# Cross attention 0 of a Perceiver block: key and value projections as three float16 matmuls, and one maximum operation over both row halves

## The chip, the cores and the metric

The kernel runs on one core of a Trainium2 chip. The metric is the device time of one execution in microseconds (us), the median of several runs. TensorE does the matmuls, VectorE (DVE), ScalarE (ACT) and GpSimd (POOL) work beside it, SyncE (SP) issues the DMAs. Each engine executes its own list of instructions in order; semaphores connect the lists.

## The reference: what is computed

The model has six parts one after the other (two cross attentions, a linear and a rotary attention, two mixtures of experts). The change is in the cross attention of the first part. The latents `x` are 32 batches of 64 rows of width 128, the context `ctx_1024` is 32 batches of 1601 rows of width 128, and there are 16 heads of width 8:

```python
def _mha_cross(x, mem, in_w, in_b, out_w, out_b):
    B, L, D = x.shape          # 32, 64, 128; mem: 32, 1601, 128
    H = NHEAD                  # 16
    hd = D // H                # 8
    ...
    q = _split_heads(x @ wq.T + bq, H)
    k = _split_heads(mem @ wk.T + bk, H)
    v = _split_heads(mem @ wv.T + bv, H)
    scores = jnp.einsum('bhqd,bhkd->bhqk', q, k) * (1.0 / math.sqrt(hd))
    attn = jax.nn.softmax(scores, axis=-1)
    out = _merge_heads(jnp.einsum('bhqk,bhkd->bhqd', attn, v))
    return out @ out_w.T + out_b
```

Everything is float32 in the reference, so the kernel either multiplies in float32 or splits a float32 number in a high and a low half of two bytes each.

## The kernel before

`cross_attention_0` goes through 16 pairs of batches. A pair `i` has four units `v` (batch `b = v // 2`, half of the heads `v % 2`), a unit has seven steps `st` of 256 context rows. In the loop of TensorE a step holds, in this order:

- `maxima`: two bf16 matmuls (line 988, contraction of 64 rows each, one into bank 0 and one into bank 1) that make scores for the row maximum of the next unit. In the loop they run two steps ahead. The seventh has 65 columns for each group of heads (line 992).
- one piece of other work, all of which shares bank 7: in units 0 and 2 a chunk of the value projection (`values`, line 948; such a unit is called a value unit below), in units 1 and 3 a chunk of the key projection (`keys`, line 942; a key unit). Chunks are 512, 512, 512 and 65 context rows and go to steps 0 to 3. Step 4 has `final`, step 6 of a key unit has `queries` (line 955). `take_bank7` makes each wait for the reader of the one before.
- `mix` (line 1029), probabilities times values, which waits for the exponentials of ACT (line 1200);
- `scores` of two steps on (line 1009); after step 5 `shifts` (lines 964 and 965), which bring the maximum into the queries.

DVE follows in the same order: two maximum reductions for each step (line 1103, one for each bank), the spreading of the maximum (lines 1108 to 1116) and the result of the unit before (lines 1136, 1138) at step 4, the shifted queries (line 1122) after step 5, the bias of the queries (line 1090) at step 6 of a key unit, and the masking of the mix (lines 1127, 1130) ahead of the first reduction of the next unit. TensorE may write bank 0 again when the reduction of bank 0 is through, and bank 1 when that of bank 1 is:

```python
for rt in range(2):
    wait_if(eng, a_max, n * 14 + 2 * a + rt - 1)
```

ACT copies key and value chunks from bank 7 (lines 1184, 1193) between the exponentials. POOL splits keys into bf16 halves (lines 897, 899) and queries (904 to 911). SP loads the context and spreads the split keys over partitions (24 DMAs for each batch). The context `ctxT` is float32 and goes straight from its DMA into the projections. Projections of pair `i + 1` are made within pair `i`. The functions as they stand before the change:

## Time and profile before

| | before |
|---|---|
| median of 3 runs | 3556.06 us (3551.76 to 3568.44) |
| the profiled execution: its own time | 3552.84 us |
| its span from first to last instruction | 3551.1 us |
| TensorE busy | 3326.5 us, 94% |
| VectorE busy | 2495.5 us, 70% |
| ScalarE busy | 1909.4 us, 54% |
| GpSimd busy | 1102.6 us, 31% |
| mean granted TensorE clock | 0.964 of 2.4 GHz |

The whole program is one chain of stages on one core. The stage of the change runs from about 172 to 1108 us of the span. The profile gives busy times for each engine, groups instructions by line, and for the idle time before an instruction it names the engine that released it. A row of the timeline has the start, the duration (of a merged group, from the first start to the last end), engine, line and operation. The end of a matmul is modelled and reaches into the next one, so the cost of a matmul in a stream is read from one start to the next.

### The profile page before, as it was taken

Reading aid. Unit: us, or ns where it says so; the run is one execution under the profiler, and the core shown is the slowest. Engines: PE = TensorE matmul, PEld = TensorE weight load, DVE = VectorE, ACT = ScalarE, POOL = GpSimd, SP = SyncE. Lnnn points to the kernel's source line nnn. Section 1 sums busy time; section 2 is a strip of 40 time slices with the busy share of each in tenths; the row PEclk is TensorE's granted clock in tenths of the full one; section 3 lists DMA queues with packets and bytes.
Section 4 is the critical chain, followed back from the end, with each engine's and each line's share of the span. In section 5 each row is a group of like instructions: output and inputs, shape, how many; then the busy total and the mean of one; then the engine's idle time right before and its main releaser. Section 6 shows DMA issues by size and latency. Waiting matters only on the chain. (4 is left out here: it accounts for less than half of the span.)

```text
span 3551.1 us, 83011 instructions
## 1 busy us (share of the span) xinstructions
PE 3326.5 (94%) x32677; PEld 2375.5 (67%) x32913; DVE 2495.5 (70%) x7178; ACT 1909.4 (54%) x2964; POOL 1102.6 (31%) x795
## 2 busy tenths in 40 slices
PE   7789999999998788999999999999999999797999
PEld 5646666666666666677777777777777777565666
DVE  6757777777775443777777777777777777577544
ACT  4336666666565232566666666666666666344333
POOL 1033333334330001444434433444344333130000
PEclk9979999999999688999999999999999999898999
DMA  1023333333320011111111111111111110100000
GB/s 54 19 64 79 72 76 76 75 82 71 75 65 10 2 48 33 43 32 43 43 33 32 43 34 32 42 43 35 31 42 43 34 31 22 48 1 28 1 1 13
DMA packets 96677, 146.45 MB, mean 41 GB/s; under 512 B 14976, under 2 KB 74400, under 8 KB 95520
## 3 DMA queue, kind: packets, MB, share of 16 engines
q1 hardware_dynamic: 96288, 141.12, 14.8%
q8 instruction: 262, 4.29, 0.5%
q14 instruction: 127, 1.04, 0.1%
HBM read 100.66 MB, written 1.05 MB: 29 GB/s over the span
## 5 line engine op out<-in xcount | busy, mean ns | idle before, releaser
L2263 DVE SCALAR_TENSOR_TENSOR arena<-banks,arena 128x512 f16<-128x512 f32 (+1 forms) x1024 | 554.5, 583 | 308.6 <-ACT arena L2352 307.2
L2352 ACT ACTIVATE arena<-banks 128x512 f16<-128x512 f32 (+1 forms) x1024 | 471.3, 512 | 400.1 <-PE banks L2170 397.1
L1103 DVE TENSOR_REDUCE arena<-banks 128x1 f32<-128x512 f32 (+1 forms) x896 | 529.7, 628 | 187.6 <-PE banks L988 182.4
L1200 ACT ACTIVATE arena<-banks 128x1024 f32<-128x1024 f32 (+1 forms) x448 | 425.1, 964 | 316.5 <-PE banks L1009 313.5
L2275 DVE CUSTOM_DVE_ANT_0 arena<-banks,arena 128x1024 f32<-128x1024 f32 (+1 forms) x512 | 494.4, 987 | 32.1 <-issue 31.9
L2359 ACT ACTIVATE arena<-arena 128x1601 f32<-128x1601 f32 x256 | 417.7, 1632 | 107.8 <-DVE arena L2281 105.8
L2170 PE MATMUL banks<-consts,arena 128*128 128x128 f32 (+1 forms) x3328 | 456.8, 275 | 7.1 <-DVE arena L2263 7.0
L2184 PE MATMUL banks<-arena 128*128 128x256 f16 (+1 forms) x1664 | 456.1, 274 | 0.7 <-ACT arena L2366 0.7
L2186 PE MATMUL banks<-arena 128*128 128x256 f16 (+1 forms) x1664 | 451.3, 271 | 0.0
L2185 PE MATMUL banks<-arena 128*128 128x256 f16 (+1 forms) x1664 | 450.2, 271 | 0.0
L2170 PEld LDWEIGHTS banks<-consts,arena 128*128 128x128 f32 (+1 forms) x3328 | 364.8, 141 | 17.3 <-issue 10.1
L2160 PE MATMUL banks<-arena 128*128 128x512 bf16 (+1 forms) x992 | 329.5, 332 | 11.6 <-POOL arena L2130 4.6
L2159 PE MATMUL banks<-arena 128*128 128x512 bf16 (+1 forms) x896 | 294.6, 329 | 4.1
L1029 PE MATMUL banks<-arena 128*32 128x192 f32 (+1 forms) x6656 | 290.3, 279 | 2.2 <-ACT arena L1200 2.1
L1029 PEld LDWEIGHTS banks<-arena 128*32 128x32 f32 x6656 | 185.7, 110 | 154.5 <-ACT arena L1200 71.8
L2161 PE MATMUL banks<-arena 128*128 128x512 bf16 (+1 forms) x948 | 286.8, 329 | 1.7
L2133 POOL TENSOR_TENSOR arena<-arena 128x1664 f32<-128x1664 f32 x32 | 120.2, 3757 | 466.0 <-ACT arena L2377 466.0
L897 POOL TENSOR_TENSOR arena<-arena,one 128x512 bf16<-128x512 f32 (+1 forms) x128 | 112.2, 877 | 414.8 <-ACT arena L1184 401.2
L988 PE MATMUL banks<-arena 64*128 64x512 bf16 x768 | 183.6, 384 | 30.8 <-DVE arena L1103 30.8
L1672 PEld LDWEIGHTS banks<-arena 128*128 128x128 f32 x1536 | 185.8, 192 | 28.4 <-DVE x L1961 9.7
L2128 POOL TENSOR_TENSOR arena<-y,one 128x1024 bf16<-128x1024 f32 x32 | 60.6, 1895 | 429.2 <-ACT y L2372 427.8
L1799 ACT ACTIVATE arena<-banks,weights,arena 128x512 f32<-128x512 f32 x128 | 99.6, 778 | 174.6 <-PE banks L1656 174.6
(360 smaller groups left out, 6119.2 us busy)
## 6 DMA issues: line engine op xcount, KB each, us to landing
arena<-in_ctxT SPq DMA_DIRECT2D x64, 800.5 KB, 4.4
arena<-arena SPq DMA_DIRECT2D x768, 50.0 KB, 2.2
arena<-in_ctx SPq DMA_DIRECT2D x32, 768.0 KB
arena<-in_mask SPq DMA_DIRECT2D x32, 200.1 KB, 4.5
arena<-in_m2w SPq DMA_DIRECT2D x3, 2048.0 KB, 8.1
arena<-in_xw SPq DMA_DIRECT2D x1, 2048.0 KB, 11.6
weights<-in_weights SPq DMA_DIRECT2D x1, 1920.0 KB, 12.2
arena<-in_ctx SPq DMA_DIRECT2D x32, 32.5 KB
```

Source lines behind the costliest of these rows:

```text
L1029: mm = eng.matmul(c.ps[HR * x:HR * x + HR, 6, a:z], v9[0:w, b, e:e + HR], pr[0:w, at % 4, rt * 512 + t2 * 256 + a:rt * 512 + t2 * 256 + z] ...
L1103: eng.tensor_reduce(o, s, AX, ALU.max).then_inc(a_max, 1)
L1200: eng.activation(pr[0:w, at % 4, :].rearrange("p (x n) -> p x n", x=2)[:, :, 0:n], c.ps[0:w, bank:bank + 2, 0:n], ACT.Exp, scale=scale).th ...
L2160: eng.matmul(o, qh[:, b, q], cl[:, b, a:z], start=False, stop=False)
L2170: mm = eng.transpose(c.ps[0:w, 4 + gr % 2, (kt % 4) * P:(kt % 4 + 1) * P], sm[:, g % 4, kt * P:kt * P + w], c.C("ident"))
L2184: eng.matmul(o, nh[0:w, b, kt, :], pth[0:w, p % 2, kt, :], start=kt == 0, stop=False)
L2185: eng.matmul(o, nh[0:w, b, kt, :], ptl[0:w, p % 2, kt, :], start=False, stop=False)
L2186: mm = eng.matmul(o, nl[0:w, b, kt, :], pth[0:w, p % 2, kt, :], start=False, stop=kt == KT - 1)
L2263: eng.scalar_tensor_tensor(out=part(ptl, g, gr), in0=turned(gr), scalar=TOP, in1=part(pth, g, gr), op0=ALU.mult, op1=ALU.subtract).then_in ...
L2275: eng.tensor_tensor_reduce(out=sm[:, g % 4, a:z], in0=src, in1=hide[:, g // T % 2, a:z], scale=1.0, scalar=-BIG, op0=ALU.add, op1=ALU.max, ...
L2352: eng.activation(part(pth, g, gr), turned(gr), ACT.Copy, scale=TOP).then_inc(t_high, 1)
L2359: eng.activation(sm[:, g % 4, :], sm[:, g % 4, :], ACT.Exp, bias=nmx[:, g % 4, :], scale=scale, accum_out=den[:, b, hp:hp + 1]).then_inc(e ...
```

## The change

It has five parts.

1. In all pairs but the first, keys and values come from three float16 matmuls each, high weights times high context, and the two products of a high with a low half, summed in bank 7. Pair 0 keeps float32.
2. The float16 halves of the context are made for each batch: ACT sums absolute values of the loaded context in each row (`magnitudes`), POOL puts the sums on a diagonal (`diagonal`), TensorE brings the diagonal to every partition (`ctx_row`, in bank 7), DVE takes the largest and makes a scale of it (`ctx_scale`, four small operations), and POOL scales, takes the high half and the low half (`split_ctx`, three operations over 1601 columns). ACT multiplies the scale out when it copies bank 7. The halves of the weights are made once at the beginning (`weights_peaks`, `weights_row`, `weights_split`).
3. DVE reduces banks 0 and 1 with one operation. `a_ps` and `a_max` count steps now, and TensorE waits once, for the reduction of both banks, ahead of the two matmuls of the next step.
4. SP issues the loads of the context in another order, each after the split of the batch that had the buffer.
5. In `spread_max` the high half of the maximum is a `tensor_tensor` with one instead of a `tensor_copy`.

The core of the diff:

```diff
 # SP
         def body(i, more):
-            if more:
-                load_ctx(i + 1, 0)
+            if i == 0 and more:
+                load_ctx(1, 0)
+            if i > 0 and more:
+                load_ctx(i + 1, 1)
             spread_keys(i, 1, 0)
             spread_keys(i, 1, 1)
+            if i == 0 and more:
+                load_ctx(1, 1)
+            if i + 2 < PAIRS:
+                load_ctx(i + 2, 0)
             if more:
-                load_ctx(i + 1, 1)
                 spread_keys(i + 1, 0, 0)
                 spread_keys(i + 1, 0, 1)
 # POOL
+        def split_ctx(i, b):
+            n = batch_no(i, b)
+            x = ctxT[:, b, :]
+            eng.wait_ge(c_inverse, n + 1)
+            eng.tensor_tensor(x, x, per_c[:, b, :].to_broadcast([P, S]), ALU.mult).then_inc(c_scaled, 1)
+            eng.wait_ge(c_scaled, n + 1)
+            if i > 1:
+                eng.wait_ge(v_ps, (i - 1) * 8 + 4 * b + 4)
+            eng.tensor_tensor(ch[:, b, 0:S], x, c.one[:].to_broadcast([P, S]), ALU.mult).then_inc(c_high, 1)
+            eng.wait_ge(c_high, n + 1)
+            eng.tensor_tensor(cl[:, b, 0:S], x, ch[:, b, 0:S], ALU.subtract).then_inc(c_split, 1)
...
         def body(i, more):
             if more:
-                for b in range(2):
-                    split_keys(i + 1, b)
-                    split_queries(i + 1, b)
+                split_keys(i + 1, 0)
+                diagonal(i + 1, 1)
+                split_queries(i + 1, 0)
+                split_ctx(i + 1, 1)
+                split_keys(i + 1, 1)
+                if i + 2 < PAIRS:
+                    diagonal(i + 2, 0)
+                split_queries(i + 1, 1)
+                if i + 2 < PAIRS:
+                    split_ctx(i + 2, 0)
 # TensorE
             if n == 0:
-                eng.wait_ge(ctx_loaded[b], i * 16 + 16)
-            a, z = chunks[n]
-            eng.matmul(c.ps[:, 7, 0:z - a], c.W("c_wk"), ctxT[:, b, a:z], start=True, stop=True).then_inc(k_ps, 1)
+                eng.wait_ge(w_low, 2)
+                eng.wait_ge(c_split, batch_no(i, b) + 1)
+            eng.matmul(o, wh[:, 0, :], ch[:, b, a:z], start=True, stop=False)
+            eng.matmul(o, wh[:, 0, :], cl[:, b, a:z], start=False, stop=False)
+            eng.matmul(o, wl[:, 0, :], ch[:, b, a:z], start=False, stop=True).then_inc(k_ps, 1)
...
+        def ctx_row(i, b):
+            n = batch_no(i, b)
+            take_bank7((c_top, n + 1))
+            eng.wait_ge(c_diag, n + 1)
+            eng.matmul(c.ps[:, 7, 2 * P:3 * P], ones, diag_c, start=True, stop=True).then_inc(c_row, 1)
...
+            wait_if(eng, a_max, n * STEPS + a)
             for rt in range(2):
-                wait_if(eng, a_max, n * 14 + 2 * a + rt - 1)
...
-                mm.then_inc(a_ps, 1)
+            mm.then_inc(a_ps, 1)
...
                     mix(i, v, st)
+                    if st == 6 and v == 1 and more:
+                        ctx_row(i + 1, 1)
+                    if st == 6 and v == 3 and i + 2 < PAIRS:
+                        ctx_row(i + 2, 0)
 # DVE
-            for rt in range(2):
-                eng.wait_ge(a_ps, n * 14 + 2 * a + rt + 1)
...
+            eng.wait_ge(a_ps, n * STEPS + a + 1)
+            if a < 6:
+                o = mxp[:, v % 2, a // 3, :, a % 3]
+                src = c.ps[:, 0:2, :]
+            else:
+                o = mxp[:, v % 2, :, :, 3].rearrange("p s r -> p r s")
+                src = c.ps[:, 0:2, 0:2 * KL].rearrange("p r (s n) -> p r s n", n=KL)
+            eng.tensor_reduce(o, src, AX, ALU.max).then_inc(a_max, 1)
...
-            eng.tensor_copy(mxs[:, :, 0], mx).then_inc(mx_high, 1)
+            eng.tensor_tensor(mxs[:, :, 0], mx, c.one[:].to_broadcast([P, 4]), ALU.mult).then_inc(mx_high, 1)
...
+        def ctx_scale(i, b):
+            n = batch_no(i, b)
+            eng.wait_ge(c_row, n + 1)
+            eng.tensor_reduce(top_c, c.ps[:, 7, 2 * P:3 * P], AX, ALU.max).then_inc(c_top, 1)
+            eng.wait_ge(range_set, 1)
+            eng.wait_ge(c_top, n + 1)
+            eng.scalar_tensor_tensor(out=floor_c, in0=top_c, scalar=1e-25, in1=per_range, op0=ALU.max, op1=ALU.mult).then_inc(c_floor, 1)
+            eng.wait_ge(c_floor, n + 1)
+            eng.reciprocal(per_c[:, b, :], floor_c).then_inc(c_inverse, 1)
+            if i > 1:
+                eng.wait_ge(v_made, (i - 1) * 8 + 4 * b + 4)
+            eng.tensor_tensor(units[:, b, :], per_top, floor_c.to_broadcast([P, 2]), ALU.mult).then_inc(c_units, 1)
...
                     if st == 6 and v % 2 == 1 and more:
                         queries(i + 1, v // 2)
+                        if v == 1:
+                            ctx_scale(i + 1, 1)
+                        elif i + 2 < PAIRS:
+                            ctx_scale(i + 2, 0)
 # ACT
+        def magnitudes(i, b):
+            eng.wait_ge(ctx_loaded[b], i * 16 + 16)
+            if i > 1:
+                eng.wait_ge(v_ps, (i - 1) * 8 + 4 * b + 4)
+                eng.wait_ge(c_diag, batch_no(i - 1, b) + 1)
+            eng.activation(ch[:, b, 0:S], ctxT[:, b, :], ACT.Abs, accum_out=total[:, b, :]).then_inc(c_total, 1)
...
                     exps(i, v, st)
+                    if i + v == 0 and st == 0 and more:
+                        magnitudes(1, 0)
+                    if st == 5 and v == 0 and more:
+                        magnitudes(i + 1, 1)
+                    if st == 5 and v == 2 and i + 2 < PAIRS:
+                        magnitudes(i + 2, 0)
```

Lines have other numbers after the change: the matmuls of `maxima` are 1069 and 1073, the key matmuls 1004 to 1006, the value matmuls 1016 to 1018, `ctx_row` 1031, the reductions 1190, `ctx_scale` 1253 to 1261, `split_ctx` 950 to 956.

DVE around the border from a key unit to a value unit, before (1122 shifted queries, 1090 bias of the queries, 1127 and 1130 masking, then the reductions of steps 0 to 3 of the next unit):

```order
L1122 CAST arena<-banks 128x256
L1103 TENSOR_REDUCE arena<-banks 128x1 x2
L1090 TENSOR_TENSOR arena<-banks,weights 128x256
L1127 TENSOR_TENSOR arena<-banks,consts 128x256
L1130 TENSOR_REDUCE arena<-arena 128x64
L1103 TENSOR_REDUCE arena<-banks 128x1 x8
```

The same place of the list of DVE after the change:

```order
L1209 CAST arena<-banks 128x256
L1190 TENSOR_REDUCE arena<-banks 128x2
L1178 TENSOR_TENSOR arena<-banks,weights 128x256
L1253 TENSOR_REDUCE arena<-banks 128x1
L1256 SCALAR_TENSOR_TENSOR arena<-arena 128x1
L1258 RECIPROCAL arena<-arena 128x1
L1261 TENSOR_TENSOR arena<-arena 128x2
L1214 TENSOR_TENSOR arena<-banks,consts 128x256
L1217 TENSOR_REDUCE arena<-arena 128x64
L1190 TENSOR_REDUCE arena<-banks 128x2 x4
```

The eight reductions have become four, and the four operations of `ctx_scale` stand ahead of the masking and of the reductions of the value unit.

POOL from the splitting of one batch's keys to that of the next, after the change (923 and 925 keys, 944 diagonal, 930 to 937 queries, 950 to 956 context):

```order
L923 TENSOR_TENSOR arena<-arena,one 128x65
L925 TENSOR_TENSOR arena<-arena 128x65
L944 TENSOR_TENSOR arena<-consts,arena 128x128
L930 TENSOR_TENSOR arena<-arena,one 128x256
L932 TENSOR_TENSOR arena<-arena,consts 128x256
L934 TENSOR_TENSOR arena<-arena 128x256
L937 TENSOR_TENSOR arena<-arena,consts 128x4x64 x2
L950 TENSOR_TENSOR arena<-arena 128x1601
L954 TENSOR_TENSOR arena<-arena,one 128x1601
L956 TENSOR_TENSOR arena<-arena 128x1601
```

Before, the list goes from the five operations on queries straight to the next keys; the diagonal and the three long operations have come between.

## Rows read from the trace of the kernel before

**Rows 1.** Busy time by stretch: start:end us, then each engine, TensorE clock, DMA

```profile
400.00:600.00 200.00, 192.36 (x2945) 121.83 (x2942) 158.36 (x341) 122.41 (x157) 71.81 (x91) 1.00 0.34 76
```

**Rows 2.** Timeline of POOL, the same place of four half pairs

```profile
474.23 0.61 POOL L904 TENSOR_TENSOR arena<-arena,one 128x256 bf16<-128x256 f32 x1 [4.03 <-DVE arena L1090]
...
557.88 0.61 POOL L904 TENSOR_TENSOR arena<-arena,one 128x256 bf16<-128x256 f32 x1 [4.03 <-DVE arena L1090]
```

**Rows 3.** Timeline of TensorE in a half pair: start us, us, operation

```profile
490.46 0.38 PE L988 MATMUL banks<-arena 64*128 64x512 bf16 x2
490.76 1.13 PE L942 MATMUL banks<-arena,weights 128*128 128x512 f32 x2
491.82 0.65 PE L1029 MATMUL banks<-arena 128*32 128x192 f32 x16
...
494.82 0.38 PE L988 MATMUL banks<-arena 64*128 64x512 bf16 x2
...
500.47 1.10 PE L955 MATMUL banks<-xT,weights 128*128 128x64 f32 x8
...
505.06 1.16 PE L948 MATMUL banks<-weights,arena 128*128 128x128 f32 x8
506.15 0.65 PE L1029 MATMUL banks<-arena 128*32 128x192 f32 x16
...
509.19 0.38 PE L988 MATMUL banks<-arena 64*128 64x512 bf16 x2
...
514.94 0.63 PE L1029 MATMUL banks<-arena 65*32 65x192 f32 x8
```

**Rows 4.** Timeline of DVE over the end of the same key unit

```profile
495.23 1.91 DVE L1103 TENSOR_REDUCE arena<-banks 128x1 f32<-128x512 f32 x4 [0.89 <-PE banks L988]
...
497.38 0.32 DVE L1110 CAST arena<-arena 128x4 bf16<-128x4 f32 x1
...
502.95 1.29 DVE L1103 TENSOR_REDUCE arena<-banks 128x1 f32<-128x512 f32 x2
```

**Rows 5.** Operations elsewhere in the kernel, by form: count, busy us, mean ns

```profile
L2715 DVE TENSOR_REDUCE arena<-banks 128x16 f32<-128x1024 f32 x16 | 19.5, 1222 | 10.7 <-PE banks L2513 10.7
L2133 POOL TENSOR_TENSOR arena<-arena 128x1664 f32<-128x1664 f32 x32 | 120.2, 3757 | 466.0 <-ACT arena L2377 466.0
L2138 POOL TENSOR_TENSOR arena<-arena 128x1664 f16<-128x1664 f32 x32 | 100.3, 3133 | 2.5
L2136 POOL TENSOR_TENSOR arena<-arena,one 128x1664 f16<-128x1664 f32 x32 | 94.7, 2958 | 2.5
L2359 ACT ACTIVATE arena<-arena 128x1601 f32<-128x1601 f32 x256 | 417.7, 1632 | 107.8 <-DVE arena L2281 105.8
```

**Rows 6.** Timeline of TensorE: two-byte matmuls in a stream

```profile
513.31 0.23 PE L964 MATMUL banks<-arena 128*128 128x128 bf16 x1
...
513.49 0.22 PE L965 MATMUL banks<-arena 128*128 128x128 bf16 x1
...
2001.06 0.38 PE L2160 MATMUL banks<-arena 128*128 128x512 bf16 x1
...
2001.92 0.38 PE L2161 MATMUL banks<-arena 128*128 128x512 bf16 x1
```

**Rows 7.** Timelines of DVE and TensorE at the entry of the stage

```profile
208.22 8.45 DVE L1103 TENSOR_REDUCE arena<-banks 128x1 f32<-128x512 f32 x13 [19.21 <-PE banks L988]
...
232.82 0.50 PE L992 MATMUL banks<-arena 64*128 64x65 bf16 x4
...
237.64 1.12 PE L942 MATMUL banks<-arena,weights 128*128 128x512 f32 x2
```

**Rows 8.** Late in the stage: five microseconds by stretch, and DVE at two borders

```profile
1030.00:1035.00 5.00, 5.00 (x43) 3.82 (x43) 3.91 (x8) 1.94 (x2) 2.87 (x5) 0.71 0.38 72
...
1031.39 0.43 DVE L1090 TENSOR_TENSOR arena<-banks,weights 128x256 f32<-128x256 f32 x1
...
1060.80 0.43 DVE L1090 TENSOR_TENSOR arena<-banks,weights 128x256 f32<-128x256 f32 x1
```

102 lines of the change are left out of this document (88 added, 14 removed).

## The prediction, made before the changed kernel ran

> **What bounds the kernel now.** The change touches one stage, so I looked first at the stage by windows: TensorE is busy 192.4 of 200 us at clock 1.00, DVE 158.4, ACT 122.4, POOL 71.8 [rows 1]. The busy share of TensorE is no proof, since ends of matmuls are modelled. So I took the period. One half pair (a key unit and a value unit) takes (557.88 - 474.23) / 3 = 27.88 us [rows 2], so any change of a half pair counts about 30 times. Then the timeline of TensorE through one half pair, cut where the engine that sets the pace changes [rows 3]. From the queries (500.47) to the maximum matmuls of step 3 (509.19) are 8.72 us, from the mix at 514.94 to the same place of the key unit (494.82 + 27.88) 7.76 us: in both the steps follow without idle time, TensorE bounds. The reader is to see two key steps from 490.46 to 494.82, 2.18 us each: 0.30 for the maximum matmuls, 1.06 (490.76 to 491.82) for the key chunk, 0.82 for mix and scores. A value chunk takes 506.15 - 505.06 = 1.09. Between, from step 3 to the next mix or queries, are 509.19 to 514.94 = 5.75 and 494.82 to 500.47 = 5.65 us. There DVE bounds: its first reduction starts 0.41 after the matmuls, four reductions take 1.91, and it has no gap until the reduction at 502.95 [rows 4]. So the half pair is 8.72 + 5.75 + 7.76 + 5.65.
>
> **The change, part by part.** *Key and value matmuls.* Full-height two-byte matmuls of 512 columns follow each other every (2001.92 - 2001.06) / 4 = 0.215 us, of 128 columns, each with its own weights, every (513.49 - 513.31) / 3 = 0.06 us [rows 6]. Three of 512 are 0.65 for 1.06, so a key chunk saves 0.41; twelve of 128 are 0.72 for 1.09, a value chunk saves 0.37. Three chunks of a unit lie in the stretch that TensorE bounds. The fourth, of 65 rows, lies under DVE's chain and saves nothing. That is 1.23 and 1.11 us, 2.34 for a half pair. For 128 columns the bounds are 0.72 and, if the weight loads set the pace, the old 1.09; I take the first, whose row has the same shape.
>
> *One reduction for two banks.* The nearest row, 128x1024 from two banks, takes 1.22 us [rows 5], two of 512 columns about 1.29. DVE gains 0.07. But TensorE may now write neither bank before both are read, and DVE starts only when both are written. Hand-over (0.41, I take 0.45 for the second matmul), reduction 1.22 and way back (0.06, an estimate) make 1.73 us as the least time from one pair of maximum matmuls to the next. With the shorter chunks a key step would be 2.18 - 0.41 = 1.77: just above it. Wherever DVE has something else in between, or the step is short, TensorE now stands.
>
> *Stretch by stretch.* Queries to step 3, 8.72 us: 1.11 less for the chunks; `ctx_row` adds a quarter of a value chunk, 0.27, and 0.14 of waiting, since bank 7 is free only when DVE has added the bias. Then DVE: the reduction of step 2 starts at 502.95, 2.48 after the queries [rows 4]. Now `ctx_scale` comes first: it can start at about 2.16, when `ctx_row` is through, and its four small operations take 0.87 (four between 0.17 and 0.32; 0.7 to 1.3 as bounds). Masking follows, the reduction starts at 3.8 and ends at 5.0. TensorE has step 1 ready at 4.37 and stands 0.7 us; before, bank 0 was free at 3.2. Sum: -1.11 + 0.27 + 0.14 + 0.7 = 0. The value chunks gain nothing.
> From the mix to step 3 of the key unit, 7.76 us: -1.23 for the chunks, and TensorE stands 0.5 instead of 0.2 us ahead of steps 0 and 1, because the reductions behind the shifted queries have one buffer: -0.9.
> The two stretches of DVE: the 65-column tile (banks 0 and 1 again) cannot be written before 1.73 after the matmuls of step 3. TensorE is there at 1.3 and stands 0.4, and the tile's reduction ends at 2.5 instead of 0.41 + 1.91 = 2.3. Against this +0.2 stand 0.05 from the next merged reduction, and in the key unit 0.15 from the mended copy: the CAST takes 0.32 there, beside POOL's work [rows 4], and its neighbours of the same size 0.17. Sum: 0, plus or minus 0.1.
> A half pair goes from 27.88 to 27.0 us. From the first keys of pair 1 to the last queries are 29.4 half pairs: **-26 us**.
>
> *The mended copy* also keeps POOL's new long operations out of the chain. First the row: a copy of 128x4 took 0.32 beside POOL and 0.17 is the size of its neighbours. The Trainium skill ("Advanced Engine Details and Errata", VectorE Performance Modes) says that the second port is shared between GpSimd and two-port copies, which block each other. A copy that had stayed could by that rule wait out an operation of 3 us, up to 2.8 more in each unit; the trace shows such a wait only in small.
>
> *Preparing the context on POOL.* Rows of the same kind over 1664 columns are 2.96 (times one, to f16) and 3.13 (difference, to f16) [rows 5]; for 1601 columns 2.85 and 3.01. With the scaling at 2.85 and three gaps the split takes 9.0 us; with all three at the dearest row (3.76, so 3.61) 11.1. It starts some 5.1 us after the queries (five operations on queries are ahead of it), ends at 14.2, and the keys are due at 16.1. So it is hidden, with 1.9 us to spare; behind POOL only the keys of TensorE wait. *ACT*: `magnitudes`, 1.63 us [rows 5] and a read of the accumulator, goes ahead of the exponentials of step 6, which are needed 2 us later than they are ready now. Hidden, barely. *SP*: the loads move among the 24 spreading DMAs of a batch; each is issued some 13 us before `magnitudes` wants it. Nothing.
>
> *Entry and end.* (a) Ahead of the first maxima are the weights' row, a float32 matmul of 256 columns, and five small DVE operations: 3 us. The reductions of the first unit took (8.45 - 0.3) / 6 = 1.36 for each step [rows 7]; with one buffer, and matmuls that take 0.6 at the lower clock, 2.0: +3.8. Together **+6.7**. (b) The first split cannot start before `ctx_scale` in unit 0. The 65-column tile is at 232.82, the spreading of the maximum and `ctx_scale` end at about 235.2, the split at 244.2. The keys were due at 237.64 [rows 7]: TensorE stands, **+6.6**. (c) The standing keeps TensorE at 1.2 GHz longer: an estimate of **+2**, two chunks at half speed. (d) In the last units there are no projections, a step is 1.1 us of TensorE and the reductions set the pace, 1.73 for 1.29; part of it hides behind the exponentials: **+2**.
>
> Sum: -26 + 6.7 + 6.6 + 2 + 2 = -8.7. The profiled execution took 3552.84 us (span 3551.1); so 3544.1. The median is 3.2 above the profiled execution: **3547 us**.
>
> **The rivals.** *The hand-overs cost nothing.* If DVE keeps up everywhere, the half pair loses 2.34 and gains only 0.41 for `ctx_row`: 1.9 x 29.4 = 56 less, 17 for entry and end: 3556 - 39 = 3517. For it: DVE idles 0.89 us ahead of step 3 [rows 4]. Against it: that gap lies in the full steps, not at the borders, where the four stands of TensorE are.
> *The clock falls.* From 1030 to 1035 us the granted clock was 0.71 on average, so at its lower level for part of it, and the half pair around took 1060.80 - 1031.39 = 29.41, 1.53 more [rows 8]. It happened with TensorE nearly always busy. After the change TensorE stands at the borders of units about 4.5 us in a half pair, by the sums above, for 2.7 now. With one drop in each half pair the time is 3547 + 46 = 3593; from 18 drops on it is slower by over 0.5%. Against it: the stretch of rows 1 ran at 1.00. The Trainium skill ("TensorE: Matmul & The Clock Gate", A second HAM failure mode: psum-queue depth-cycling) describes such a case, where short idle times between groups of matmuls that cycle through PSUM make the clock swing.
> *Value matmuls are bound by their weights.* At the old 1.09 for a chunk the value units lose 1.1 instead of nothing, +33: 3580; halfway, 3563. For it: twelve in a row with new weights each, where the row has four. The Trainium skill (same page, Back-to-back issue gap) gives 81 ns for 128 columns in a stream of loads and matmuls; by it a chunk would be 0.97, and the estimate 3565. The trace has 60 ns.
> *POOL is late.* If the split takes over 10.9 us, each further us costs 29: 3576 at 11.9. Against it: the two f16 rows.
>
> **How the numbers follow.** A measurement of this kernel tells 0.5%, some 18 us, from nothing. Chances: forecast 0.47, its own range 3530 to 3563 (reduction spaced 1.15 or 1.22, small operations at their bounds); no hand-over cost 0.22; clock 0.15; value matmuls 0.10; POOL 0.06. Faster takes the second case and the lower edge of the first, 0.30; slower the clock, POOL and the upper half of the value case, 0.25; the rest 0.45. The range goes to 3517 and 3580.
>
> **What would show it.** Right: half pairs of 27.0 us; key chunks of 0.65 and value chunks of 0.72; idle time of TensorE ahead of line 1069 in step 1 of value units (0.7) and of line 1073 (0.4), both released by line 1190; reductions of 1.22; a stand of 6 to 7 us ahead of the first line 1004, released by POOL line 956; later ones not. It would be wrong if the half pair is near 26 (hand-over), if drops of the clock repeat, or if line 1004 waits for POOL in every pair.

## The result, and the profile after

The kernel before took 3554.9 us (median of 4 runs, 3551.76 to 3568.44), the changed one 3668.72 us (median of 4, 3665.53 to 3672.54): 1.0313 times as long, with a 95% interval of 1.0284 to 1.0342. The forecast was 3547 and its range ended at 3580. The change makes the kernel 114 us slower.

First the stretch of [rows 1], and POOL's first operation on the queries as in [rows 2], now line 930:

```profile
400.00:600.00 200.00, 167.30 (x2759) 103.63 (x2751) 154.28 (x236) 124.65 (x156) 126.46 (x107) 0.94 0.30 68
```

```profile
491.84 0.61 POOL L930 TENSOR_TENSOR arena<-arena,one 128x256 bf16<-128x256 f32 x1 [3.44 <-DVE arena L1178]
...
584.83 0.61 POOL L930 TENSOR_TENSOR arena<-arena,one 128x256 bf16<-128x256 f32 x1 [3.44 <-DVE arena L1178]
```

TensorE is busy 167.3 of 200 us where it was 192.4, at a mean granted clock of 0.94 where it was 1.00: it has less to do, and stands. A half pair takes (584.83 - 491.84) / 3 = 31.0 us, for 27.88 before and 27.0 forecast. Over the 29 half pairs from the third on the mean is 31.15 (before 27.94): 93 of the 119 us between the two profiled spans (3670.5 and 3551.1). The first two half pairs, 38.83 and 40.81 for 30.17 and 31.91, bring 17.6; the rest of the kernel, ahead of and behind the stage, some 9.

Where does a half pair lose 3.2 us? The timelines of DVE, of POOL and of TensorE at the end of a value unit, at the place where [rows 4] shows a key unit:

```profile
502.18 0.17 DVE L1195 TENSOR_REDUCE arena<-arena 128x4 f32<-128x16 f32 x1
502.39 1.70 DVE L1197 TENSOR_TENSOR arena<-arena,one 128x4 bf16<-128x4 f32 x1
504.12 0.17 DVE L1199 TENSOR_TENSOR arena<-arena 128x4 bf16<-128x4 f32 x1
...
501.04 3.02 POOL L956 TENSOR_TENSOR arena<-arena 128x1601 f16<-128x1601 f32 x1
...
503.23 0.65 PE L1110 MATMUL banks<-arena 128*32 128x192 f32 x16
505.46 0.23 PE L1045 MATMUL banks<-arena 128*128 128x128 bf16 x1 [1.58 <-DVE o L1225]
...
506.72 0.39 PE L1069 MATMUL banks<-arena 64*128 64x512 bf16 x2 [0.86 <-DVE arena L1190]
...
508.81 0.61 PE L1004 MATMUL banks<-arena 128*128 128x512 f16 x1
509.22 0.63 PE L1005 MATMUL banks<-arena 128*128 128x512 f16 x1
...
512.15 0.39 PE L1004 MATMUL banks<-arena 128*128 128x512 f16 x1
512.38 0.38 PE L1005 MATMUL banks<-arena 128*128 128x512 f16 x1
```

The reader is to compare two ends. The mended copy (line 1197), four elements in each partition, ends at 502.39 + 1.70 = 504.09; POOL's low half (line 956) ends at 501.04 + 3.02 = 504.06. The next operation of the same size takes 0.17. It is so everywhere in the stage: 41 of the 63 copies started beside an operation of POOL that ran on for longer than 0.17 us, and each of the 41 ended 0.02 to 0.03 us behind it; the other 22 took 0.17 or 0.18. So the copy waits 1.5 us, TensorE stands 1.58 ahead of the shifts (line 1045) and 0.86 more ahead of the maxima behind them, and the keys, 2 us later, run at half speed: 0.41 us from matmul to matmul at 508.81, 0.23 at 512.15. The stretches of that place show the clock:

```profile
508.00:510.00 2.00, 1.80 (x14) 0.43 (x7) 1.93 (x4) 1.94 (x2) 0.00 (x0) 0.66 0.26 104
510.00:512.00 2.00, 2.00 (x27) 1.05 (x26) 0.37 (x1) 0.91 (x2) 0.83 (x1) 0.50 0.00 0
512.00:514.00 2.00, 2.00 (x31) 0.92 (x29) 1.23 (x1) 1.75 (x3) 1.51 (x3) 0.99 0.00 0
```

The clock is the last figure but two: 0.50 is the lower of the two levels, 1.2 GHz. Such a fall, 3.4 us long (three times 6.8), begins in each of the 29 half pairs from the third on, 16.4 to 18.6 us after the queries, behind the first of these two stands. The other place that lost is behind the queries, where the forecast had `ctx_scale` and a stand of TensorE in step 1 (DVE, then TensorE):

```profile
492.34 0.29 DVE L1253 TENSOR_REDUCE arena<-banks 128x1 f32<-128x128 f32 x1 [0.58 <-PE banks L1031]
492.74 0.42 DVE L1256 SCALAR_TENSOR_TENSOR arena<-arena 128x1 f32<-128x1 f32 x1
493.19 0.16 DVE L1258 RECIPROCAL arena<-arena 128x1 f32<-128x1 f32 x1
493.27 0.70 DVE L1261 TENSOR_TENSOR arena<-arena 128x2 f32<-128x2 f32 x1
493.89 0.41 DVE L1214 TENSOR_TENSOR arena<-banks,consts 128x256 f32<-128x256 f32 x1
...
494.41 0.65 PE L1110 MATMUL banks<-arena 128*32 128x192 f32 x16 [0.55 <-issue]
...
495.90 0.39 PE L1069 MATMUL banks<-arena 64*128 64x512 bf16 x2 [0.52 <-DVE arena L1190]
```

Two of the four take 0.42 and 0.70 where the reciprocal takes 0.16; POOL runs its operations on the queries at that time. `mix` of step 0 needs bank 6, which line 1214 reads until 494.30: that is where the 0.55 come from that the profile calls "issue".

I cut the half pair as the prediction did (from the queries to the maximum matmuls of step 3, to the mix of step 6, to step 3 of the key unit, to the queries; starts on TensorE, typical half pairs, most of them between 600 and 710 us; those of the last four rows have no fall of the clock):

| kernel | queries to step 3 | to mix | to step 3 | to queries | half pair |
|---|---|---|---|---|---|
| before | 8.72 | 5.75 | 7.76 | 5.65 | 27.88 |
| forecast | 8.72 | 5.75 | 6.86 | 5.65 | 27.0 |
| after | 9.63 | 7.31 to 7.56 | 8.2 | 5.64 to 5.91 | 31.1 |
| low half behind the shift | 9.62 | 5.79 | 7.17 | 6.04 | 28.62 |
| the same, scale frozen | 8.11 | 5.78 | 7.17 | 6.04 | 27.10 |
| the same, one input in ctx_scale | 8.87 | 5.78 | 7.17 | 6.04 | 27.86 |
| before with one reduction | 8.71 | 5.80 | 7.95 | 5.61 | 28.07 |

The last four are experiments, below.

### The profile page after: what moved, and what is told of

The parts are those of the page before. It is cut to its first block and busy times, and to the rows that moved or that the text cites. A ratio compares the mean times of both kernels' runs of the same rounds, so it can differ in the third digit from the quotient of the medians.

```text
span 3670.5 us, 84402 instructions
## 1 busy us (share of the span) xinstructions
PE 3319.3 (90%) x33485; PEld 2353.0 (64%) x33485; DVE 2558.5 (70%) x6862; ACT 1972.1 (54%) x3024; POOL 1379.6 (38%) x916
## 5 line engine op out<-in xcount | busy, mean ns | idle before, releaser
L1190 DVE TENSOR_REDUCE arena<-banks 128x2 f32<-128x1024 f32 (+1 forms) x448 | 497.2, 1110 | 197.3 <-PE banks L1069 174.1
L2313 PE MATMUL banks<-arena 128*128 128x512 bf16 (+1 forms) x1024 | 343.2, 335 | 5.2 <-POOL arena L2284 5.2
L2314 PE MATMUL banks<-arena 128*128 128x512 bf16 (+1 forms) x1024 | 341.3, 333 | 0.0
L1110 PE MATMUL banks<-arena 128*32 128x192 f32 (+1 forms) x6656 | 302.3, 287 | 19.2 <-issue 15.8
L2315 PE MATMUL banks<-arena 128*128 128x512 bf16 (+1 forms) x1024 | 315.2, 333 | 0.0
L1110 PEld LDWEIGHTS banks<-arena 128*32 128x32 f32 x6656 | 193.1, 112 | 153.8 <-issue 51.3
L1069 PE MATMUL banks<-arena 64*128 64x512 bf16 x768 | 158.1, 408 | 81.2 <-DVE arena L1190 81.2
## 6 DMA issues: line engine op xcount, KB each, us to landing
weights<-in_weights SPq DMA_DIRECT2D x1, 1920.0 KB, 12.2
```

Of the source, the lines that this page charges most:

```text
L1110: mm = eng.matmul(c.ps[HR * x:HR * x + HR, 6, a:z], v9[0:w, b, e:e + HR], pr[0:w, at % 4, rt * 512 + t2 * 256 + a:rt * 512 + t2 * 256 + z] ...
L1190: eng.tensor_reduce(o, src, AX, ALU.max).then_inc(a_max, 1)
L2313: eng.matmul(o, qh[:, b, q], ch[:, b, a:z], start=True, stop=False)
```

## The experiments

Each ratio is to the kernel before, timed beside the run on the same chip. "Half pair" is the distance from one bias of the queries on DVE to the next, read over the 29 from the third on. "A fall of the clock" is a stretch at the lower level in the trace's record of the granted clock.

### POOL's split cut to 64 columns

```diff
+            w = 64
-            eng.tensor_tensor(ch[:, b, 0:S], x, c.one[:].to_broadcast([P, S]), ALU.mult).then_inc(c_high, 1)
+            eng.tensor_tensor(ch[:, b, 0:w], x[:, 0:w], c.one[:].to_broadcast([P, w]), ALU.mult).then_inc(c_high, 1)
...
```

All three operations of the split are cut so, and the low half is set to zero once: work is left out, and keys and values of later pairs come out wrong.

> The changed kernel, but the three POOL operations of split_ctx work on 64 of the 1601 columns (the rest of the low half is set to zero once), so keys and values of later pairs are left wrong; everything else is issued as it was. Theory PORT: a DVE operation with two inputs in SBUF waits until the POOL operation that is running has ended (the conversion of the maximum took 1.70 and 1.94 us where the last operation of split_ctx ran), and the clock falls behind that stand of TensorE. Then the conversion is 0.17 us in every unit, the half pair loses 1.6 us of waiting and the drop of the clock (about 1.5 us): 31.05 becomes 27.9 to 28.3, and about 9 us of the stand ahead of the first keys go too: 3560 to 3580 us. Theory ONE BUFFER: the merged reduction costs the time, POOL is beside the point: the half pair stays near 31, 3650 to 3665 us.

Measured: 3598.05 us, ratio 1.0128 (1.0102 to 1.0154), half pairs of 28.63. Of the 114 us 71 are gone, with the same matmuls, reductions and `ctx_scale`. In the value units the copy takes 0.17. But in the key units, which come at another phase of POOL now, it waits, beside an operation of 512 columns:

```profile
609.83 0.64 DVE L1199 TENSOR_TENSOR arena<-arena,one 128x4 bf16<-128x4 f32 x1
...
609.28 1.17 POOL L925 TENSOR_TENSOR arena<-arena 128x512 bf16<-128x512 f32 x1
```

Again both end together (610.47 and 610.45). The load of the split on POOL is the larger part of the loss; 1.6 us of a half pair above the forecast are still there. The clock still falls in 12 of 29 half pairs, early in them and, but for one, at a price of at most 0.23 us.

### Two reductions again

Part 3 of the change undone: for each step two matmuls with a wait each, two reductions, 14 hand-overs for 7.

```diff
-            wait_if(eng, a_max, n * STEPS + a)
             for rt in range(2):
+                wait_if(eng, a_max, n * 14 + 2 * a + rt - 1)
...
```

> The changed kernel with part 3 undone: two reductions for each step, one for each bank, TensorE waits for each bank by itself. Theory PORT: the wait of the conversion and the drop of the clock stay; only the stands ahead of steps 1 and of the 65-column tile go, some 0.7 + 0.4 + 0.3 us in a half pair: 29.5 to 30.3, 3630 to 3650 us. Theory ONE BUFFER: the half pair falls below that of before, to 26 to 27.5: 3520 to 3570 us.

Measured: 3666.61 us, ratio 1.0319 (1.0293 to 1.0345), the same as after. The stand ahead of the maxima behind the shifts falls from 0.86 to 0.33, but those ahead of the shifts (1.47) and of the mix (0.54) stay, and the half pair is 31.1 on average, as after. While the copy waits for POOL, the merged reduction costs the loop nothing. At the entry it does: the first half pair is 36.15 for 38.83.

### One reduction alone

The kernel before with part 3 only.

```diff
-                eng.tensor_reduce(o, s, AX, ALU.max).then_inc(a_max, 1)
+            eng.tensor_reduce(o, src, AX, ALU.max).then_inc(a_max, 1)
...
```

> The kernel before with part 3 alone: one reduction over both banks, float32 projections, nothing new on POOL, ACT or SP. Theory PORT: with full-length chunks the step (2.18 us) is longer than hand-over, reduction and way back (1.73), only the borders of units lose: half pair 27.9 to 28.4, 3556 to 3575 us. Theory ONE BUFFER: half pair 29.5 or more, 3610 us or more.

Measured: 3566.78 us, ratio 1.0034 (1.0022 to 1.0047). Half pairs of 28.07, 0.2 more, all of it in the third stretch of the table, where TensorE stands 0.86 and 0.20 ahead of the maxima behind the shifts; four half pairs of 29 have a fall of the clock. So with chunks of full length the one buffer costs 0.2 there, for which the forecast had 0.3, and no gain of DVE pays it back. With the falls and the entry that makes 12 us, not 114.

### The split in quarters

Each of the three operations in four of some 400 columns, twelve for three: the same work, short pieces.

```diff
-            eng.tensor_tensor(cl[:, b, 0:S], x, ch[:, b, 0:S], ALU.subtract).then_inc(c_split, 1)
+            for a, z in zip(cuts, cuts[1:]):
+                last = eng.tensor_tensor(cl[:, b, a:z], x[:, a:z], ch[:, b, a:z], ALU.subtract)
+            last.then_inc(c_split, 1)
...
```

> The changed kernel, each of the three operations of split_ctx cut into four of about 400 columns, same work. Theory PORT: the DVE operation waits at most for the rest of one short operation, 0.8 us instead of up to 3: the conversion 0.2 to 0.9 us in value units, half pair 28.3 to 30.3 depending on whether the clock still falls: 3590 to 3640 us, although POOL works 0.6 us longer on a split. If the wait were for the end of all of split_ctx (a queue, or a semaphore), the conversion still takes 1.7 to 2.3 us and the time is 3668 to 3685. Theory ONE BUFFER: no change, 3665 to 3675.

Measured: 3674.09 us, ratio 1.0345 (1.0316 to 1.0373), no better. DVE, and POOL's group of four at the same time:

```profile
626.65 0.44 DVE L1204 TENSOR_TENSOR arena<-arena,one 128x4 bf16<-128x4 f32 x1
627.12 0.82 DVE L1206 TENSOR_TENSOR arena<-arena 128x4 bf16<-128x4 f32 x1
627.98 0.88 DVE L1210 TENSOR_TENSOR arena<-consts,arena 128x64 bf16<-128x64 f32 x1
...
626.17 3.45 POOL L962 TENSOR_TENSOR arena<-arena 128x401 f16<-128x401 f32 x4
```

The copy takes only 0.44, but now the two behind it wait as well, one of POOL's pieces each, and take 0.82 and 0.88. That is 1.57 in sum above the 0.17, 0.17 and 0.23 of an idle POOL, as much as with one long operation. This is the most telling run: the wait is not the copy's alone; each of the three, all with two inputs in SBUF, waits for the piece of POOL's that is running, and cutting POOL's work does not help where three such operations follow each other.

### The low half behind the shift

Nothing is left out; POOL waits once more, until DVE has made the shift of the next unit.

```diff
             eng.wait_ge(c_high, n + 1)
+            eng.wait_ge(l_made, unit_no(i - 1, 1 if b == 0 else 3) + 1)
             eng.tensor_tensor(cl[:, b, 0:S], x, ch[:, b, 0:S], ALU.subtract).then_inc(c_split, 1)
```

> The kernel after, with one wait more on POOL: the third operation of the split (the low half) starts only when the shift of the next unit's maxima has been multiplied out on VectorE, so that no operation of 1601 columns runs while spread_max does. Nothing is left out. Port theory: the conversion that took 1.70 and 1.94 us takes 0.17 in every half pair, the low half runs from about 503.1 to 506.1 and is still in time for the keys at about 508, TensorE's idle ahead of the shifts (1.58) falls to about 0.2, and the fall of the granted clock behind it goes too. Half pairs from 31.1 to between 27.6 (both gone) and 29.3 (only the wait gone); time 3668.7 less 29 x 1.8 to 3.5, 3567 to 3616, most likely near 3590. Rival, transfers and keys late: the later low half holds up the keys of the next unit or the next load of the context, TensorE stands ahead of the keys by 1 us or more, and the time stays above 3640. Rival, one large tile: what costs is the whole load on VectorE and the single tile of the maxima, not the wait; time stays above 3650.

Measured: 3596.6 us, ratio 1.0128 (1.0103 to 1.0152): 72 us back for one wait. Half pairs of 28.62, and one of 29 is longer by over 0.6 us. DVE, POOL and TensorE:

```profile
622.89 0.17 DVE L1198 TENSOR_TENSOR arena<-arena,one 128x4 bf16<-128x4 f32 x1
...
623.67 3.25 POOL L957 TENSOR_TENSOR arena<-arena 128x1601 f16<-128x1601 f32 x1 [2.39 <-DVE arena L1204]
...
624.44 0.23 PE L1046 MATMUL banks<-arena 128*128 128x128 bf16 x1
...
625.70 0.39 PE L1070 MATMUL banks<-arena 64*128 64x512 bf16 x2 [0.86 <-DVE arena L1191]
```

No idle time is left ahead of these shifts, those of the value unit (1.58 in the kernel after). The second stretch is back at 5.79, and the third falls by 1.0, since its keys run at full clock. So of the 2.5 us that one wait gives back, about 1.5 to 1.8 are the wait and 1.0 the clock; the fourth stretch loses 0.4 at most, from a copy that takes 0.64 beside POOL's keys. The keys were not late, though the low half ends 2.5 us later than it had: 14.8 us after the first operation on the queries, for 12.2.

The clock has not stopped falling. It does so in 11 of 29 half pairs, in one of them behind the shifts of the value unit (29.50 us), in ten at another place, 1.3 to 2.1 us after the queries. TensorE's stands at the end of the key unit, and the stretches of one such fall:

```profile
608.96 0.23 PE L1046 MATMUL banks<-arena 128*128 128x128 bf16 x1 [0.42 <-DVE o L1226]
...
610.09 0.39 PE L1070 MATMUL banks<-arena 64*128 64x512 bf16 x2 [0.73 <-DVE arena L1191]
```

```profile
612.00:614.00 2.00, 1.95 (x25) 1.23 (x22) 1.28 (x5) 0.79 (x1) 1.68 (x3) 0.63 0.22 37
614.00:616.00 2.00, 2.00 (x26) 1.58 (x28) 1.97 (x4) 1.70 (x3) 1.92 (x4) 0.52 0.44 83
```

The clock stands last but two: 0.63 and 0.52. These ten cost 0.07 to 0.19 us each. Behind `ctx_scale` TensorE stands 0.54 and 0.52 in the other half pairs, and in this one not at all: it was slower and would have waited anyway. The same fall costs more below, where that wait is shorter.

### The queries of POOL behind the scale as well

```diff
             eng.wait_ge(q_made, n)
+            if i > 0 and (b == 0 or i + 1 < PAIRS):
+                eng.wait_ge(c_units, 2 * i + b)
...
```

> As the run before it in this call (low half behind the shift), and POOL's four operations on the queries wait until the four small operations of ctx_scale are through, since these took 0.42 and 0.70 beside them where 0.17 would do. Port theory: ctx_scale gives back 0.7 to 0.8 us of VectorE once each half pair, the conversion stays at 0.17, and TensorE's idle in step 1 of the value units (0.52) and ahead of the first maxima step (0.86) shrink; half pairs 0.3 to 0.8 below those of the run before it, time 10 to 25 us below it, the nearest to the forecast of 27.0 per half pair. Rival: the queries come 1.3 us later and with them the split, whose low half now ends after 508.8, so that the keys wait and the time is the same or up to 20 us above.

Measured: 3601.06 us, ratio 1.0129 (1.0111 to 1.0148), no gain. The small operations take 0.16, 0.16 and 0.14 as expected, and the first stretch is 8.81 for 9.62. But everything on POOL comes later, and the high half now lies on the copy (0.87 in the value units): the second stretch is 6.48 for 5.79. The half pair is 28.50, and in ten of 29 it is 29.3 to 29.4, since the clock falls again behind the shifts of the value unit, where TensorE stands 0.75 and 0.86. The expectation had looked at the keys for the price of the delay, and it was in the copy and in the clock.

### The kernel before, with idle work on POOL

Float32 projections, plain copy, two reductions; after the queries of each half pair POOL runs three operations of the split's size on buffers of its own.

```diff
                     split_queries(i + 1, b)
+                    spare_split(2 * i + b)
...
```

> The kernel before, with its float32 projections and its plain copy, and nothing of the change but POOL's load: after the queries of each half pair POOL runs three operations on 1601 columns of a spare buffer (8.9 us), which nothing waits for. Port theory: the conversion of the maxima (plain copy, 0.17 before) takes up to 2 us wherever one of the three runs beside it, TensorE stands about 1.6 ahead of the shifts and its granted clock falls there; before's half pair of 27.88 grows by 1.6 to 3.3, the time by 48 to 95 us: 3600 to 3650. In the kernel before the queries end at a slightly different time, so the wait may be anything between 0.2 and 2.9. Rival, POOL's operations are covered by VectorE's single-tensor work: nothing grows by over 0.2, time 3555 to 3562.

Measured: 3687.61 us, ratio 1.0376 (1.0357 to 1.0394): 132 us more, beyond the expected 95. DVE, POOL, TensorE:

```profile
619.88 2.62 DVE L1124 CAST arena<-arena 128x4 bf16<-128x4 f32 x1
...
619.45 3.02 POOL L924 TENSOR_TENSOR arena<-arena 128x1601 f16<-128x1601 f32 x1
...
623.88 0.23 PE L978 MATMUL banks<-arena 128*128 128x128 bf16 x1 [2.37 <-DVE o L1152]
```

```profile
626.00:628.00 2.00, 2.00 (x26) 1.25 (x22) 1.48 (x4) 0.61 (x1) 0.00 (x0) 0.50 0.43 179
628.00:630.00 2.00, 2.00 (x4) 0.50 (x2) 1.29 (x2) 1.33 (x2) 0.00 (x0) 0.50 0.00 0
```

Nobody waits for these three operations by a semaphore, and still they cost more than the whole change: 2.45 us of waiting, and then TensorE at its lower level in these windows and parts of the two around them. Half pairs alternate between 31.7 and 33.1, so 1.4 to 2.8 us come on top of the wait.

### The plain copy

```diff
-            eng.tensor_tensor(mxs[:, :, 0], mx, c.one[:].to_broadcast([P, 4]), ALU.mult).then_inc(mx_high, 1)
+            eng.tensor_copy(mxs[:, :, 0], mx).then_inc(mx_high, 1)
```

> The kernel after, with the old copy of the maxima (a plain conversion with one input) in place of the mended one (a multiplication by a row of ones). Theory that every operation of VectorE with two inputs or a double-speed mode waits: the same, 3663 to 3674, the copy itself 1.7 and 1.9 in the value units. If a copy with one input and 4 columns doesn't wait, the wait moves to the subtraction behind it (two inputs), 1.5 to 1.7 there, and the time is again the same. Theory that the plain copy waits longer than the mended one (the reason given for the change): 3675 or more, with a copy of over 2.0 us.

Measured: 3668.31 us, ratio 1.0324 (1.0304 to 1.0344), as with the mended copy. The plain copy takes the same 1.70 and 1.95 in the value units. The mending changes nothing.

### Two reductions, without the wait

The kernel with the low half behind the shift, and part 3 undone as above.

> The kernel with the low half behind the shift (3596.6 us), with part 3 undone: two reductions with a wait of their own for each step of the maxima. In that kernel TensorE still stands 0.86 and 0.73 us ahead of maxima steps that follow a shift, where the kernel before stood about 0.2 and 0.2. Theory that the one tile's hand-over is now on the path, since the wait on POOL's low half is gone: these two stands fall below 0.4 each, half pairs from 28.65 to 27.7 to 28.3, time 3568 to 3588. Theory that the reductions themselves fill VectorE there (the same columns, one fixed part more per step): the same within 6 us, 3590 to 3603.

Measured: 3600.53 us, ratio 1.0139 (1.0123 to 1.0155). The stands of 0.86 and 0.73 are gone (0.31 and 0.20), but the half pair is 28.6 as it was, and nine of 29 are longer by over 0.6 us. The third stretch is 7.13 with two reductions and 7.17 with one: behind the shifts DVE's reductions hold TensorE up either way. The theory that the hand-over is on the path falls a second time.

### One input in ctx_scale

The kernel of the run above (low half behind the shift, two reductions), and:

```diff
-            eng.scalar_tensor_tensor(out=floor_c, in0=top_c, scalar=1e-25, in1=per_range, op0=ALU.max, op1=ALU.mult).then_inc(c_floor, 1)
+            eng.tensor_scalar(floor_c, top_c, 1e-25, 1 / TOP, ALU.max, ALU.mult).then_inc(c_floor, 1)
-            eng.tensor_tensor(units[:, b, :], per_top, floor_c.to_broadcast([P, 2]), ALU.mult).then_inc(c_units, 1)
+            eng.tensor_scalar(units[:, b, :], per_top, floor_c[:, 0:1], None, ALU.mult).then_inc(c_units, 1)
```

> As the run before it in this call, and the two operations of ctx_scale that took 0.42 and 0.70 us (two inputs each: a scalar-tensor-tensor with a tensor of the range, a multiplication by a broadcast column) written with one tensor input and a number or a column as the scalar; same result. Port theory, by which only operations with two inputs in SBUF wait for POOL's running one: they take 0.17 each beside the same POOL operations, 0.75 us of each half pair comes back, time 15 to 25 us below the run before it. Rival, any small operation of VectorE waits beside POOL: 0.4 and 0.7 as they were and no change of the time over 5 us. A float32 operation with one input may also run at a faster mode that waits as well; then the same as the rival.

Measured: 3587.32 us, ratio 1.0093 (1.0078 to 1.0108), 13 us below the run above for 15 to 25 expected. DVE, beside POOL's same operations on the queries:

```profile
614.12 0.15 DVE L1258 TENSOR_SCALAR arena<-arena 128x1 f32<-128x1 f32 x1
614.39 0.21 DVE L1263 TENSOR_SCALAR arena<-arena 128x2 f32<-128x2 f32 x1
...
613.73 0.61 POOL L932 TENSOR_TENSOR arena<-arena,consts 128x256 f32<-128x256 bf16 x1
614.43 0.76 POOL L934 TENSOR_TENSOR arena<-arena 128x256 bf16<-128x256 f32 x1
...
815.98 0.69 DVE L1263 TENSOR_SCALAR arena<-arena 128x2 f32<-128x2 f32 x1
...
815.92 0.73 POOL L934 TENSOR_TENSOR arena<-arena 128x256 bf16<-128x256 f32 x1
```

0.15 for 0.42 and 0.21 for 0.70. The first ran through while POOL's line 932 did (613.73 to 614.34), and took 0.153 on average in all 30 places. The second, with two columns, only missed POOL: it started at 614.39, between two operations. In seven of the 30 places it started while line 934 ran; there it took 0.24 to 0.69 and ended 0.02 to 0.03 behind it, as at 815.98. So one input is enough for a wait with two columns, and the expectation's last rival, an operation with one input that waits as well, holds for this one. The half pair without a fall is 27.85; twelve of 29 are longer by over 0.6. Here the fall of 3.4 us just after the queries costs 0.9.

### The scale frozen

The kernel with the low half behind the shift; `ctx_row` and `ctx_scale` return at once from the third batch on, so this work is left out and the scale of the second batch is used.

```diff
             n = batch_no(i, b)
+            if n > 1:
+                return
...
```

> The kernel with the low half behind the shift (3596.6 us), with ctx_row on TensorE and the four operations of ctx_scale on VectorE left out from the third batch of the context on: the scale found for the second batch serves for the rest. Everything else, magnitudes, diagonals, splits and the f16 projections, stays. What it tells: how much of the 28.65 per half pair is the scale's machinery on VectorE and in bank 7. Theory: VectorE loses 1.6 us of work plus 0.6 of waiting for ctx_row between the queries' bias and the first steady maxima step, where the half pair stands 2.35 us above before; 1.4 to 2.3 come back, half pairs 26.4 to 27.3, time 3530 to 3556. Rival, TensorE is the bound there and VectorE's work fills its slack: under 0.5 per half pair, time 3582 to 3597.

Measured: 3573.75 us, ratio 1.0068 (1.0052 to 1.0084), short of the expected 3530 to 3556. The half pair without a fall is 27.10, as expected, 1.52 less, all in the first stretch (9.62 to 8.11). But 17 of 29 half pairs are longer by over 0.6 us, up to 29.74, by falls of the clock: on average 0.52 of the 1.52 us is left.

### One reduction, low half behind the shift, one input

The kernel with the low half behind the shift, and `ctx_scale` as above; nothing is left out.

> The kernel with the low half behind the shift and one reduction per step (3596.6 us; its half pair is 9.62 from queries to step 3, 5.79, 7.17 and 6.04 us), and the two operations of ctx_scale with one tensor input. By the runs so far these give back 0.8 us of the first stretch (8.83) and touch no other: half pairs of 27.85, the same as before the change, time 3570 to 3577; it would stand above before by the entry alone (17 us) and so be no version worth having. If this kernel shows the falls of the clock that its sister with two reductions showed in 12 of 29 half pairs, 3582 to 3590; if merged reductions and one-input operations together let TensorE run on, below 3565.

Measured: 3591.76 us, ratio 1.0107 (1.0089 to 1.0126). The undisturbed half pair is 27.86, as worked out; ten of 29 have a fall, which costs 0.8 to 1.0 us, or 2.3 where it is 6.8 long. The time is 2 us above the range that the expectation gave for a kernel with falls. None of the versions reaches the kernel before.

## Why the prediction was wrong

**The step that failed** is "The mended copy also keeps POOL's new long operations out of the chain", and with it "behind POOL only the keys of TensorE wait". The step before it had read the row rightly: 0.32 for 0.17 beside POOL's work [rows 4]. What it made of it was wrong twice. First, it took the wait for a trait of the plain copy, by the rule of the Trainium skill ("Advanced Engine Details and Errata", VectorE Performance Modes). Second, it did not ask what the row waits for. That stands in the kernel before itself (DVE at 497.38, [rows 4], and POOL):

```profile
497.38 0.30 POOL L897 TENSOR_TENSOR arena<-arena,one 128x65 bf16<-128x65 f32 x1
```

The CAST ends at 497.70 and POOL's operation at 497.68, and it is so in all 30 places where it took 0.32; with an operation of 1601 columns in that place the same CAST took 2.62 (the kernel before with idle work on POOL). In the kernel after the plain and the mended copy wait alike (1.70 and 1.70), and the wait takes in the subtraction and the multiplication behind them (0.82 and 0.88 with the split in quarters). The mended copy has gained a second input, the row of ones. The Trainium skill has the wider rule on another page ("SBUF — State Buffer", Who interferes with whom): an operation of VectorE with both inputs in SBUF contends with one of GpSimd that reads SBUF, and the one that is blocked waits for the whole instruction. The trace agrees (504.09 and 504.06, and 41 such copies of 41). The prediction rested on the narrower sentence alone. And the argument about POOL asked only whether the split is ready in time, where it was right to 0.3 us: the split starts 5.1 us after TensorE's queries (495.18 and 490.10), takes 2.86, 2.86 and 3.02 and ends at 14.0, and in the steady half pairs no key waits for it. That a short operation of DVE can wait for a long one of POOL without any semaphore between them was priced in one sentence (2.8 us in each unit), as a fate that the change avoids, and did not become a rival.

**The sum, term by term.** *Stretch from step 3 to the mix*: forecast 5.75, measured 7.31 to 7.56, the copy's wait of 1.5 to 1.8. The run with one wait more on POOL gives 5.79: the term was right but for the wait.

*From the mix to step 3 of the key unit*: forecast 6.86, measured 8.2. 1.0 of it is the lower clock, gone with the wait (7.17); the other 0.3 is a mis-sized chunk. From the start of a key chunk to the start of the mix are 0.75 us (512.15 to 512.90), not the 0.65 of three matmuls in a row: 0.31 saved and not 0.41, three times, makes 7.76 - 0.93 + 0.3 = 7.13. The other term of that stretch, 0.3 for the one buffer, is not shown by its removal: with two reductions the stretch is 7.13, with one 7.17.

*From the queries to step 3*: forecast 8.72, measured 9.63. Value matmuls follow each other every (524.69 - 524.06) / 11 = 0.057 us, as the chosen row had it, and the rival on their weights falls; a step is 1.90 for 2.21 before, so 0.31 is saved for 0.37. The stand in step 1 is 0.52 for 0.7. But `ctx_scale` takes 1.63 us from 492.34 to 493.97 for 0.87, by two waits for POOL of some 0.8 together, and then the mix of step 0 stands 0.55 for bank 6, which the forecast had not followed. With one-input operations the stretch is 8.87, 0.15 from the forecast.

*The last stretch*: 5.65 forecast, 5.64 to 5.91 measured.

**The rivals.** *The clock falls* was named, with 0.15: it was to come from short stands spread over the borders. In the kernel after it stands behind one idle time of 1.58 us and a second of 0.86, and when the first is removed and the second stays, the fall at that place goes in 28 of 29 half pairs. Falls behind short stands, as the rival had them, are those just after the queries in the versions without the long stand (0.42 and 0.73 with the low half behind the shift). In the kernel after the fall cost 1.0 us in a half pair (8.2 for 7.17), 1.53 in [rows 8].

*The hand-overs cost nothing* was half right: undoing part 3 gains nothing in the loop of any version of the changed kernel, and its own cost in the kernel before is 12 us.

*POOL is late* and *value matmuls bound by weights* did not happen. In the latter the working has a slip: a chunk of 0.97 adds 0.25 us three times in a half pair, 22 us, and gives 3569 and not 3565. In the entry, 3 and 3.8 make 6.8 and not 6.7.

**Entry and end.** Forecast 15.3 us of entry, measured 17.6 in the first two half pairs. The term for the weights was short: the timeline of TensorE has a stand of 5.69 where 3 us were given for the weights (DVE's seven operations take 4.9 us there, beside POOL's on the keys), and the term of 3.8 for the one buffer was too long, since two reductions give back 2.7 there (36.15 for 38.83). The first split's stand was too long as well (3.42 for 6.6). The +2 at the end can't be told from noise: from the last bias of the queries to the end of the span are 2490.3 us before and 2494.3 after, and between 2485.2 and 2499.7 in the versions with the low half behind the shift. The first row is that of the queries, from which the split's start is counted above:

```profile
490.10 1.10 PE L1036 MATMUL banks<-xT,weights 128*128 128x64 f32 x8
...
213.88 0.61 PE L1069 MATMUL banks<-arena 64*128 64x512 bf16 x2
220.18 0.61 PE L1069 MATMUL banks<-arena 64*128 64x512 bf16 x2 [5.69 <-DVE arena L1190]
...
259.10 0.59 PE L1004 MATMUL banks<-arena 128*128 128x512 f16 x1 [3.42 <-POOL arena L956]
```

**The account.** In the loop 27.0 became 31.1: +1.5 to 1.8 the copy's wait, +1.0 the clock behind it, +0.9 the waits of `ctx_scale` and what they delay, +0.3 the key chunks, and 0.1 in the last stretch; 4.1 us by 29 half pairs turn the forecast's -26 into +93. Even with the long wait and those of `ctx_scale` gone the change does not pay. The half pair of 27.86 is that of before, since the 1.86 us that six f16 chunks save are spent: 0.76 on finding the scale (8.87 less 8.11), 0.3 more in the same stretch, 0.3 behind the shifts, where TensorE waits for DVE's reductions with one buffer and with two, 0.4 in the last stretch on the copy's wait for POOL's keys. And 17 us of entry stay.

**What stays open.** Once the long stand is gone, the clock falls in 11 of 29 half pairs with the low half behind the shift, in 13 with POOL's queries delayed too, and in 10 to 20 in the last four runs. Nearly all of these falls begin 0.6 to 2.4 us after the queries, or behind the stands of 0.75 and 0.86 where POOL's queries are delayed. Their number hardly tells the versions apart; what they cost does, for one of 3.4 us just after the queries: 0.07 to 0.19 us with the low half behind the shift, 0.8 to 1.0 with one reduction and one input, 1.2 to 1.3 with the scale frozen. The runs don't show what sets the number. It limits what can be said of gains of half a us: the frozen scale shows 1.52 us in the undisturbed half pair and 0.5 in the mean. Nor was it tried to give the shift a form in which none of its operations waits.

## What to carry to other kernels

Before work is moved to POOL, look at what VectorE does at that hour: an operation of four columns that takes its inputs from SBUF can wait for the whole of POOL's running operation, and no semaphore, no busy share and no order of instructions shows it. The sign in the trace is a tiny operation whose duration varies (0.17 here, 0.32 there) and ends with one of POOL's; ask what it will be when POOL's operation is ten times as long. If the work must be there, a wait that holds POOL until the chain's small operations are through is worth more (72 us here) than cutting POOL's work into pieces (nothing). Then look where POOL's work has moved to: a second such wait freed `ctx_scale` and put the high half on the copy, for no gain.

## What the runs showed of the hardware

- Operations of DVE on 1 to 64 columns with two inputs in SBUF took up to 1.94 us beside a POOL operation of 1601 columns and 0.64 beside one of 512, and ended with it to 0.03 us in the pairs shown. A plain conversion of 128x4 did too (2.62). Reductions (0.17 in 59 places beside POOL), the reciprocal of one column and an operation of one column with numbers (0.15) did not. With two columns even one input waited, in the kernel with one input in `ctx_scale` in all seven places where POOL's line 934 was running (0.24 to 0.69), and in the kernel after at the entry (DVE, POOL: 215.27 and 215.25). By the Trainium skill ("Advanced Engine Details and Errata", VectorE Performance Modes) the mode that takes the second port wants source and destination in SBUF and the outermost size even in both, or odd, above one and the same in both; two and four columns meet that and one does not. The rows agree.

```profile
214.44 0.83 DVE L1238 TENSOR_SCALAR arena<-arena 128x2 f32<-128x2 f32 x1
...
214.21 1.04 POOL L923 TENSOR_TENSOR arena<-arena,one 128x512 bf16<-128x512 f32 x1
```

- The wait is for one instruction of POOL: three in a row beside pieces of 400 columns took 0.44, 0.82 and 0.88, for 0.17, 0.17 and 0.23 alone.
- An idle time of TensorE of 1.58 or 1.8 us and one of 0.86 right behind it were followed by a stretch at the lower clock level in each of 29 half pairs; at the same place 0.86 without the first was, in one of 29 (low half behind the shift). Stands of 0.42 and 0.73 at the end of the key unit were followed by one in ten of 29.
- What a stretch at the lower level costs depends on who sets the pace in it: 3.4 us of it cost 0.07 to 0.19 us where TensorE would else have stood for DVE (low half behind the shift), 0.9 at the same place where `ctx_scale` is shorter (one input), and 1.0 behind the copy's wait.
